# Count stage of a graph kernel: one-hot sets of thirty items in six groups instead of twenty in four

## The reference

```python
edge_index = jnp.stack([src, dst])
h = jnp.maximum(_layernorm(x, axis=-1), 0.0)
x = x + _L0_gnn_ref(h, qW, kW, vW, src, dst)            # attention: exp(q.k), normalised over src
h = jnp.maximum(_layernorm(x, axis=-1), 0.0)
x = x + _L1_gnn_ref(h, p_t, Wv, bv, edge_weight, edge_index)   # softmax of edge weights by dst
h = jnp.maximum(_layernorm(x, axis=-1), 0.0)
x = x + _L2_gnn_ref(h, src, dst, W, b)                   # segment_sum(h[src], dst)
h = jnp.maximum(_layernorm(x, axis=-1), 0.0)
x = x + _L3_gnn_ref(h, edge_index, w2, b2, w3, b3, w4, b4, ...)  # Chebyshev terms, mixing, batch norm
```

## Time and profile before

| what | value |
|---|---|
| median of three runs | 1190.76 us (1189.02 to 1191.69) |
| the profiled execution's own time | 1189.85 us |
| its span, first to last instruction | 1187.9 us, so 1.95 us lie around it |
| TensorE matmuls busy | 1017.8 us, 86% of the span |
| VectorE busy | 888.2 us, 75% |
| ScalarE busy | 605.4 us, 51% |
| GpSimd busy | 488.9 us, 41% |
| count loop, first to last set | about 31 to 360 us of the span |

### The profile page before, as it was taken

The page is one execution under the profiler, slowest core; times in us unless marked ns, Lnnn a source line. Parts: engine busy times, 40 slices in busy tenths (PEclk is TensorE's granted clock), DMA queues, the critical chain, the costliest instruction groups (busy, mean ns, idle before and its releaser), DMA issues.

```text
span 1187.9 us, 23158 instructions
## 1 busy us (share of the span) xinstructions
PE 1017.8 (86%) x8352; PEld 623.3 (52%) x8352; DVE 888.2 (75%) x1338; ACT 605.4 (51%) x816; POOL 488.9 (41%) x518
## 2 busy tenths in 40 slices
PE   3887777778879599999999999987997899998983
PEld 2554555445545322222233333334587799998873
DVE  8768887888665489999999999978656464533576
ACT  7556556555653399898989898851000000000321
POOL 8545433532100089999999999840000000000000
PEclk9879888887788889999999999988999799999996
DMA  0010000000001811212122222220000000010201
GB/s 8 27 42 10 5 6 5 6 9 6 15 1 48 247 41 43 68 42 69 43 66 45 70 58 66 67 69 1 1 28 34 25 35 10 2 40 8 84 17 41
DMA packets 98906, 44.79 MB, mean 38 GB/s; under 512 B 85196, under 2 KB 96716, under 8 KB 98672
## 3 DMA queue, kind: packets, MB, share of 16 engines
q1 hardware_dynamic: 97104, 41.58, 13.2%
q0 software_dynamic: 1696, 1.74, 0.5%
HBM read 30.73 MB, written 12.56 MB: 36 GB/s over the span
## 4 chain that ended last, share of the span: by engine, by line
PE 77%; issue 8%; DVE 7%; ACT 3%; POOL 3%; DMA 2%; SPq 1%; DVEq 0%; ACTq 0%; POOLq 0%
PE PS L1299 17%; PE PS L1065 12%; PE PS L553 11%; PE PS L1075 11%; PE PS L557 8%; PE PS L1739 3%; PE PS L1307 3%; PE PS L1054 3%; ACT Eb L1117 2%; PE PS L1290 1%; POOL Eb L978 1%; DVE Eb L1136 1%; PE PS L878 1%; PE PS L1746 1%; PE PS L1729 1%
## 5 line engine op out<-in xcount | busy, mean ns | idle before, releaser
L1136 DVE TENSOR_TENSOR Eb<-Eb,PS 128x2048 f32<-128x2048 f32 (+4 forms) x175 | 342.1, 2014 | 20.8 <-POOL Eb L978 10.6
L1117 ACT ACTIVATE Eb<-PS,small 128x1024 f32<-128x1024 f32 (+4 forms) x350 | 333.6, 1004 | 37.2 <-PE PS L1065 32.3
L978 POOL TENSOR_SCALAR Eb<-Eb 128x1024 f32<-128x1024 f32 (+4 forms) x350 | 318.9, 935 | 79.1 <-ACT Eb L1117 75.3
L593 ACT ACTIVATE CT<-PS 128x500 f32 x313 | 183.8, 587 | 143.4 <-PE PS L557 135.6
L553 PE MATMUL PS<-mov,oneS 128*128 128x100 f16 x1565 | 185.3, 232 | 76.8 <-issue 71.7
L553 PEld LDWEIGHTS PS<-mov,oneS 128*128 128x128 f16 x1565 | 147.1, 108 | 159.6 <-issue 114.6
L1299 PE MATMUL PS<-hs,CT 128*128 128x192 f16 (+1 forms) x2500 | 213.4, 247 | 3.6 <-DVE SG L1540 1.6
L1299 PEld LDWEIGHTS PS<-hs,CT 128*128 128x128 f16 (+1 forms) x2500 | 208.0, 99 | 7.3 <-DVE SG L1540 2.3
L1065 PE MATMUL PS<-Qb,Kb 96*128 96x512 f16 (+3 forms) x700 | 180.8, 362 | 14.5 <-DMA Kb<-kd 10.2
L435 DVE TENSOR_TENSOR oneS<-iotaX,KL 128x2560 f16<-128x2560 int16 x80 | 120.5, 1506 | 72.2 <-PE PS L557 69.6
L1075 PE MATMUL PS<-Eb,V 128*25 128x512 f32 (+3 forms) x1400 | 166.9, 549 | 0.8 <-DVE Eb L1136 0.8
(11 more groups left out here) (273 smaller groups left out, 892.4 us busy)
## 6 DMA issues: line engine op xcount, KB each, us to landing
Kb<-kd SPq DMA_DIRECT2D x168, 96.0 KB, 2.3
qd<-QH SPq DMA_DIRECT2D x12, 192.0 KB, 3.0
kd<-QH SPq DMA_DIRECT2D x12, 192.0 KB, 3.2
hs<-t_d SPq DMA_DIRECT2D x12, 192.0 KB, 2.6
Qb<-qd SPq DMA_DIRECT2D x4, 384.0 KB, 3.6
CT<-x_d SPq DMA_DIRECT2D x1, 1200.0 KB, 9.2
x_d<-B SPq DMA_DIRECT2D x6, 192.0 KB, 1.8
t_d<-A SPq DMA_DIRECT2D x6, 192.0 KB, 1.8
```

The costliest lines, as they stand in the source:

```text
L593: a.activation(K.CT[:, :, bass.ds(words[g % 4][0], GI * W)], K.bank(g % 4)[:, 0:25 * GI * W].rearrange("p (a c) -> p a c", a=25), ACT.Copy ...
L978: g.tensor_scalar(e, e, EHI, ELO, ALU.min, ALU.max).then_inc(S("clamped"), 1)
L1117: a.activation(e, ps, ACT.Exp, scale=K.unsc[0:r, :]).then_inc(S("score_exp"), 1)
L1136: v.tensor_tensor(e, e, cn, ALU.mult).then_inc(S("weighed"), 1)
```

## The change

Six groups, thirty items, make a set, so there are 53 sets; a block keeps its 120 items and now has four sets. One read of offsets on TensorE brings thirty words instead of twenty, one on ScalarE six instead of four. Both one-hot instructions of VectorE cover thirty items. The tables that place the other work by set number are scaled to the new numbers. Groups, their matmuls, their PSUM banks and their waits on ScalarE stay as they are.

```diff
@@ -99,24 +99,26 @@
 GI = 5
-SETS = 80
-SET = 4 * GI
-BLOCK = 6 * SET
+GPS = 6
+SPB = 4
+SETS = 53
+SET = GPS * GI
+BLOCK = SPB * SET
 SLOTS = NJ * BLOCK
-PRESENT = [g for g in range(4 * SETS) if GI * (g // 2) < (LH, NI - LH)[g % 2]]
+PRESENT = [g for g in range(GPS * SETS) if GI * (g // 2) < (LH, NI - LH)[g % 2]]
 INDEX = {g: i for i, g in enumerate(PRESENT)}
 DEEP = 2
 RING = 4
 
-HIGH_AT = {3 if j == 1 else 6 * (j - 1) + 1: j for j in range(1, NJ)}
-TURN_AT = {4 if j == 1 else 6 * (j - 1) + 3: j for j in range(1, NJ)}
+HIGH_AT = {2 if j == 1 else SPB * (j - 1): j for j in range(1, NJ)}
+TURN_AT = {2 if j == 1 else SPB * (j - 1) + 1: j for j in range(1, NJ)}
 
 PARTS = ((0, 1), (1, 8), (8, NJ))
 PAST_AT = {0: (0, 1, 2, 3), 1: (4, 5, 6)}
-SUM_AT, SLOTS_AT, TABLE_AT = 2, 5, 7
-
-SOFT_GAPS = (1, 1, 1, 3, 3, 1, 1, 1, 3, 3, 1, 3, 1, 3, 3, 1, 1, 1, 3, 3, 1, 1, 1, 1, 3, 3, 1)
-SOFT_AT = {16 + sum(SOFT_GAPS[:k]): k for k in range(len(SOFT_GAPS))}
+SUM_AT, SLOTS_AT, TABLE_AT = 1, 3, 5
+
+SOFT_GAPS = (1, 1, 1, 2, 2, 1, 1, 1, 2, 2, 1, 2, 1, 2, 2, 1, 1, 1, 2, 2, 1, 1, 1, 1, 2, 2, 1)
+SOFT_AT = {11 + sum(SOFT_GAPS[:k]): k for k in range(len(SOFT_GAPS))}
@@ -453,10 +455,10 @@ build_vector
     for s in range(SETS):
-        j, o = s // 6, SET * (s % 6)
+        j, o = s // SPB, SET * (s % SPB)
         v.wait_ge(S("items"), j + 1)
         if s >= DEEP:
-            v.wait_ge(S("counted"), before(4 * (s - DEEP) + 4))
+            v.wait_ge(S("counted"), before(GPS * (s - DEEP + 1)))
@@ -478,16 +480,16 @@ load_windows
-    n = SET // 4 // every
+    n = GI // every
     return [[x if k == 0 else x.with_bounds(min_val=0, max_val=(GI - 1) * W) for k, x in enumerate(vals[n * r:n * r + n])]
-            for r in range(4)]
+            for r in range(GPS)]
@@ -541,12 +543,12 @@ build_tensor
     for g in PRESENT:
-        s, o = g // 4, GI * (g % 4)
-        if g % 4 == 0:
+        s, o = g // GPS, GI * (g % GPS)
+        if g % GPS == 0:
             words = vals = to = None
             words = load_windows(K, t, mybir.EngineType.PE, s, 1)
             t.wait_ge(S("one_hot"), s + 1)
-        vals = words[g % 4]
+        vals = words[g % GPS]
@@ -574,7 +576,7 @@ build_scalar, keep_items
         if j >= RING:
-            a.wait_ge(S("one_hot"), 6 * (j - RING) + 6)
+            a.wait_ge(S("one_hot"), SPB * (j - RING + 1))
@@ -586,13 +588,13 @@ build_scalar
-        s = g // 4
-        if g % 4 == 0:
+        s = g // GPS
+        if g % GPS == 0:
             words = load_windows(K, a, mybir.EngineType.Activation, s, GI)
```

More of the change, by code:

```diff
@@ L558, in build_tensor @@
                  ).then_inc(S("counted"), 1)
-        if g == PRESENT[-1] or g // 4 != PRESENT[INDEX[g] + 1] // 4:
+        if g == PRESENT[-1] or s != PRESENT[INDEX[g] + 1] // GPS:
             if s == SUM_AT:
@@ L588, in build_scalar @@
     for i, g in enumerate(PRESENT):
-        s = g // 4
-        if g % 4 == 0:
+        s = g // GPS
+        if g % GPS == 0:
             words = load_windows(K, a, mybir.EngineType.Activation, s, GI)
         a.wait_ge(S("counted"), i + 1)
-        a.activation(K.CT[:, :, bass.ds(words[g % 4][0], GI * W)],
+        a.activation(K.CT[:, :, bass.ds(words[g % GPS][0], GI * W)],
                      K.bank(g % 4)[:, 0:25 * GI * W].rearrange("p (a c) -> p a c", a=25), ACT.Copy).then_inc(S("placed"), 1)
-        if g == PRESENT[-1] or s != PRESENT[i + 1] // 4:
+        if g == PRESENT[-1] or s != PRESENT[i + 1] // GPS:
             if s in TURN_AT:
```

## The result

The changed kernel takes 1349.44 us (median of four runs, 1348.07 to 1352.97) against 1189.89 for the kernel before in the same session. The ratio is 1.135, with a 95% interval of 1.133 to 1.137: 13% slower, 160 us, where 18 us less were forecast.

What follows compares the result with a forecast made beforehand. The prediction took TensorE's register reads between sets of groups to pace the count stage, not VectorE. Its terms, -21.4 - 1.4 - 1.8 + 6.3 = -18.3 us, gave 1171.6, as a median 1172.5 us, range 1157 to 1187.

Steps and rivals of the forecast that it cites:

- What bounds the kernel: Count stage, up to 360 us: TensorE loops through a 1.36 us read and four groups; VectorE is not the bound.
- Term 1: TensorE's register reads in the count stage: 53 of 1.652 us instead of 80 of 1361 ns, a gain of 21.4 us.
- Term 2: What surrounds a read at TensorE's set starts: 0.05 us each, 27 fewer starts, a gain of 1.4 us.
- term 3: VectorE's one long piece, the reciprocal: about 0.7 of its 2.5 us stall of TensorE stays, a gain of 1.8 us.
- Term 4: TensorE's granted clock in the count stage: half-clock share grows from 30% to 38% with longer silences, a loss of 6.3 us.
- The edits costed at nothing: Moved keys, transposes, gathers, edge loads and store in the count stage: still covered, no cost; nothing changes behind the stage.
- Words are dear: Rival for TensorE's reads: 68 ns each added word, 2042 ns a read, clock at half for 60% of sets; 1202 us, chance 0.07.
- The clock worsens: Rival for TensorE's clock: each longer silence brings half clock for the whole next set, +29 us; 1195 us, chance 0.05.
- The read is split: Rival for TensorE's reads: thirty words need two reads of 15 words a set, 129 us in all; 1214 us, chance 0.04.
- VectorE becomes the bound: Rival in the count stage: VectorE's pieces sit denser, in 38 sets, up to 5 us of stalls; 1178 us, chance 0.04.

Runs made afterwards that it cites:

- the price list: The kernel before with sixteen further TensorE reads of varied length and start behind the count stage's last group, their words used by small matmuls: 1239.06 us (one run).
- pad30: The changed kernel with its table laid out at 32 words a set, so all thirty-word reads start at a multiple of 16 bytes: 1223.35 us, ratio 1.029.
- pad32: As pad30, but TensorE reads all 32 words a set, two of them padding: 1220.09 us, ratio 1.026.

## Why the prediction was wrong, point by point

**What bounds the kernel** held: the stage is paced by the read and the groups, and each read's end is followed by the next set's first weight load.

**Term 1, the reads, is the step that failed.** It drew a line through two reads of different kinds, 20 adjacent aligned words on TensorE and 4 words five apart on ScalarE, and read the difference as 29 ns a word over a start of 780. By the price list the first is five fours, 0.08 + 5 x 0.256 = 1.36, the second four single words, 0.9 to 1.0; the line has no meaning. Both bounds were drawn from the same mistake: 1361 and 2042 ns, where 2360 and 7080 came. The term went from -21.4 to +139. The 896 ns for 4 words in rows 5 was a row for the truth, 224 ns a word; I set it aside because a proportional price at 68 ns "would make them 272", instead of asking why the two prices differ.

The Trainium skill's sentence ("Runtime: NRT & Kernel Launch", Instruction fetch mechanics) of about 200 ns a register was weighed and dismissed by the 20-word row. The runs side with it for reads that go word by word, about 233 ns each from SBUF, and against it for aligned fours, 64 ns a word. The estimate of 178 us of reads, from the 20-word read plus ten words at that price, was low as well: the measured 248 are half the sets at 236 ns a word and half at 79, and neither working told the two kinds apart.

**Term 2**, 1.4 us, and **term 3** can't be seen in the time beside this. Of term 3 the durations held: one-hots of 2156 and 1716 ns stand on the page where 2.15 and 1.71 were worked out. Its sum mixed two things, a measured stall of 2.5 and a modelled one of 0.7; like for like the room grows by 1.1 us, from 3.57 to 4.64. In the runs the reciprocal stalled nobody. In the changed kernel the waits put TensorE's silence behind it, 6.4 us, down to the one-hots, but these were done at 417.53. A 7.08 us read had begun at 411.0 and ended last, and TensorE's next set began at 418.09:

```profile
PE PS L555 <- DVE mov L437: 6.4, 1, 6.4
...
408.86 5.03 DVE L357 RECIPROCAL A<-A 128x782 f32<-128x782 f32 x1
...
415.82 1.71 DVE L437 TENSOR_TENSOR mov<-iotaM,KL 128x3000 f16<-128x3000 int16 x1
```

In pad30 and pad32, whose reads are short, no wait for one-hots follows the reciprocal either.

**Term 4, the clock, had the right sign and mechanism and was mis-sized**: 6.3 us forecast, 22 measured with silences of 2.1 and 6.9 us and a clock of 0.68, under the 0.75 that the prediction named as a sign of being wrong. Even with reads no longer in sum than before (pad32) filling the silences was worth 33 us, against the 14 of the working. That the share of half clock grows about as the silence does was not the main fault: in pad32 it went from 30% to 48% for a silence of 1.86 instead of 1.05. The price was. 48% of 53 sets are 25 sets' worth, 18 us at 0.70 each, and 33 came back. The 0.70 came from sets at half clock to their end, where part of the read hides behind slow matmuls (0.61 us idle). In pad32 the half clock took the first groups, about 0.2 us each for four of them, and the set ended at full clock with its read in the open, 1.86 and 1.83 us idle. It took nearly every set, where before the change sets ran eight in a row without one.

**The edits costed at nothing** were free as far as the waits show: behind the stage the time moved by 1.7 us in 827, and no wait for keys, edges or the store stands out. KL came later, as the prediction had allowed for: VectorE waited for it once, 6.0 us instead of 2.6. In the changed kernel that lay under a 7.08 us read of TensorE's (58.2 to 65.3 us), and in pad32, where it is 5.7 us, TensorE's waits show none for one-hots. Pad30 has one of 1.3 us, at 47.71.

**The rivals.** "Words are dear" had the right side and the right mechanism (read longer, clock lower), at 0.07 and with a price capped at 68 ns a word. "The clock worsens" was the second cause. "The read is split" did not happen: the 53 sets have 53 reads on TensorE, each of thirty words. "VectorE becomes the bound" did not either. No case had alignment in it.

## What to carry to other kernels

Before a price is drawn through two rows, ask whether they are the same kind of operation: adjacent or strided, aligned or not; a row that doesn't fit the line is the finding. Here a register read from SBUF was cheapest a word with its start at a multiple of 16 bytes and its length in whole fours, pads included; a maximum far from the median in a view of one line means that two kinds are mixed there. A silence of TensorE costs more than its length when the granted clock falls behind it; work of no use in its shadow can pay.

## What the runs showed of the hardware

- A read of words from SBUF into registers of TensorE's sequencer: 0.08 us to start, 0.256 for each aligned four, about 0.233 for each single word; a start 4 or 8 bytes off a multiple of 16, or a stride, makes all of it single words (20 words: 1.36 or 4.73 us). ScalarE's strided reads cost 0.90 us for four words and 1.31 for six, 0.31 for four adjacent aligned ones.
- The stage with one silence of 1.8 us in each set of 6.8 ran at a granted clock of 0.76, with one of about 1 us in each 4.1 at 0.85; with matmuls in the silence at 1.00 and 0.99.
- A shift or mask on TensorE's sequencer, 36 ns in the trace, made the loop 0.10 us longer.
